# First round of turned attention scores: where the mask, the keys' products and the maxima's products stand around the turn of the row maxima

## The chip, the cores and the metric

The kernel runs on one core of a Trainium2 chip. The metric is the device time of one execution in microseconds (us), median of three runs. The engines are named as in the profile: PE is TensorE's matmul stream, PEld its weight loads, DVE VectorE, ACT ScalarE, POOL GpSimd, SP SyncE with its DMA queue.

## The reference

The program is a decoder of four layers on x of 8 batches x 256 tokens x 256 features, with a context of 8 x 77 x 256. Each layer adds an attention, a cross attention and a feed-forward part to x. The parts that the change touches are four softmax attentions with 16 heads each:

```python
def _local_attn(q, k, v, window):          # L1_attn, causal, 256 tokens (two windows of 128)
    ...
    sim = jnp.einsum('bnwd,bnkd->bnwk', qw, bk)
    sim = jnp.where(mask[None], sim, -1000000000.0)
    attn = jax.nn.softmax(sim, axis=-1)
    out = jnp.einsum('bnwk,bnkd->bnwd', attn, bv)

def _mha(xq, xk, xv, Wq, bq, Wk, bk, Wv, bv, Wo, bo, causal):   # L1_xattn
    ...
    w = jax.nn.softmax(scores, axis=-1)
    out = jnp.einsum('bhqk,bhke->bhqe', w, v)
    ...
h = _mha(x, x, x, Wq1, bq1, Wk1, bk1, Wv1, bv1, Wo1, bo1, causal=True)
out = _mha(h, encoder_k, encoder_v, Wq2, bq2, Wk2, bk2, Wv2, bv2, Wo2, bo2, causal=False)
```

L2_xattn is a plain cross attention to the 77 context rows. L3_xattn is the same on features of 32 per head, exp(z) and exp(-z) side by side.

## The kernel before, in words

Each engine has one program written out by hand; what joins them are semaphores. The stages follow each other as L0_attn, L0_xattn with L0_ffn, L1_attn, L1_xattn with L1_ffn, L2_attn, L2_xattn, L2_ffn with L3_attn, L3_xattn, L3_ffn. An attention stage works in steps, one batch (256 tokens, two tiles of 128) each; L1_xattn has 16 steps, 8 causal ones (the self attention, called a) and 8 cross ones (b), in the order a0 a1 a2 b0 a3 b1 a4 b2 a5 b3 a6 b4 a7 b5 b6 b7. In a step p the engines work on `now` (scores and softmax), `last` (outputs of the step before), `soon` (projections of the next one).

What a step does for its softmax, in this order:

- Scores with the queries on the partitions, `pair_scores_tensor` (L515 for the mask, L531, L537, L545, L552 for the products), two rounds for a cross step and three for a causal one, in the four PSUM banks HI to HI+3. After each round DVE takes the row maxima, `pair_tops_vector` (L567), and raises `top`. These scores are then overwritten.
- DVE splits the maxima into three bf16 parts in four short operations, `split_tops_vector` (L576 to L582), each of which raises `part`.
- PE turns the parts with two transposes, `turn_tops_tensor` (L590), ACT copies the result from PSUM to SBUF as mT, `turn_tops_scalar` (L597).
- PE computes the scores again, now with the keys on the partitions, in the same four banks, `turned_scores_tensor`, again two or three rounds. A round consists of the mask (causal only, four matmuls of 128x512 in bf16, L515 through `hide_later`), and for each `place` (one of the four heads of a group, with its columns) four small matmuls on four row groups that subtract the maxima (`k.pick` x mT in bf16, L606, "the maxima's products") and four that multiply keys and queries in f32 (L613, "the keys' products"). Round 0 of a causal step has four places of 128 columns, a round of a cross step two places of 256 columns. After the round `t_ps` is raised and ACT takes the exponential of all four banks at once, `turned_probs_scalar` (L648), which raises `prob`. The next round waits for it, as its banks are the same.
- PE multiplies with the values, `pair_outputs_tensor` (L660, L665), ACT copies (L673), PE turns the outputs back (L682), DVE divides (L692, L694, raises `o`), PE turns them again (L701) and projects them (L414, the shared projection helper).

Around the place of the change, PE's order in the four stages is this. L1_attn: own_k for `soon`, then the turn and round 0, then the second half of the feed-forward's first product, round 1, own_v for `soon` (DVE's L761 waits for it, and behind it DVE has the two layernorms of `last`, L1954 to L1967). L1_xattn: pair_back (L682), the turn and round 0, then, if `soon` is causal, own_v (which waits for DVE's L724, the keys of `soon`) and the query, else L701 and the query; then round 1. L2_xattn: L682, turn, round 0, L701 (waits for `o` of L694), query, round 1. L3_xattn: L4132, turn, round 0, L4206 (waits for `o` of L4198), a value projection, round 1; later L4147 waits for ACT's L4179.

Signals: `after(pe, s, u, name, i)` waits for the i-th raising of `name` of step u. PE executes in order, so that everything behind a wait stands still.

Of the kernel before, what the change touches and what calls it, by code (L numbers as in the profile page):

```python
# [22 lines left out]
P = 128  # L23
B, SEQ, D = 8, 256, 256
TILES = B * SEQ // P
SPARE = 4
KC = D // P
CTX = 77
# [151 lines left out]
def cut(ap, **sizes):  # L180
    (name, n), = sizes.items()
    return ap.rearrange(f"p ({name} f) -> p {name} f", **{name: n})
# [313 lines left out]
def keys_of(s, u):  # L496
    return s.kT[u.at][:, :, 0:2 * (SEQ if u.a.causal else CTX)]


def after(eng, s, u, name, i=1):  # L500

    if u is not None:
        eng.wait_ge(*s.sig.at(u.a.p + name, 0, u.n, i))


def group(i):
    return slice(PAD * i, PAD * (i + 1))
# [89 lines left out]
    k.nc.scalar.activation(s.mT, k.ps[:, b, at:at + P].bitcast(BF16), ACT.Copy).then_inc(*s.sig.up(u.a.p + "mT"))  # L597


def turned_pair(k, s, u, c, q, keys, at, fresh):  # L600

    n = q.stop - q.start
    for ab in (0, 1):
        j, out = 2 * c + ab, slice(at + ab * n, at + (ab + 1) * n)
        for i in range(4):
            k.nc.tensor.matmul(k.ps[0:u.a.nk, HI + i, out], k.pick[group(i), j * P:j * P + u.a.nk], s.mT[group(i), q],  # L606
                               start=fresh, stop=False, skip_group_check=True)
        if u.a.wide:
            kT, qT = s.kT[u.at][:, j, keys], s.qT[u.at][:, j, q]
        else:  # L610
            kT, qT = cut(keys_of(s, u)[:, c, :], half=2)[:, ab, keys], s.qT[u.at][:, c, q]
        for i in range(4):
            ins = k.nc.tensor.matmul(k.ps[0:u.a.nk, HI + i, out], kT[group(i)], qT[group(i)], start=False, stop=True,  # L613
                                     skip_group_check=True)
    return ins


def turned_scores_tensor(k, pe, s, u, r):

    if r == 0:  # L620
        after(pe, s, u, "mT")
    else:
        after(pe, s, u, "prob", r)
    every, later, first, second = slice(0, SEQ), slice(P, SEQ), slice(0, P), slice(P, SEQ)
    if not u.a.causal:
        ins = turned_pair(k, s, u, r, every, slice(0, CTX), 0, True)
    elif r == 0:
        for i in range(4):
            hide_later(k, k.ps[:, HI + i, :], mask_of(k, "keyC"))
        for c in range(KC):  # L630
            ins = turned_pair(k, s, u, c, later, second, c * SEQ, False)
    else:
        for i in range(4):
            hide_later(k, cut(k.ps[:, HI + i, :], slot=4)[:, 0::2, :], mask_of(k, "keyC")[:, 0:2 * P])
        ins = turned_pair(k, s, u, r - 1, every, first, 0, False)
    ins.then_inc(*s.sig.up(u.a.p + "t_ps"))


# [218 lines left out]
def L2_xattn_tensor(k, pe, s):  # L857
    for p in range(B + 1):
# [19 lines left out]
            logits_tensor(k, pe, s.ahead, 0, 0, 4)  # L878
        if now:
            after(pe, s, soon, "zT")  # L880
            turn_tops_tensor(k, pe, s, now, 3)
            turned_scores_tensor(k, pe, s, now, 0)
        if last:
            after(pe, s, last, "o")
            after(pe, s, soon, "kv")
# [230 lines left out]
def L1_xattn_tensor(k, pe, s):  # L1116
    quant, _, _ = fp8_times(s)
    ends, one = len(s.steps) - 1, s.ahead
    for p in range(ends + 1):
# [29 lines left out]
        if now:  # L1149
            if soon and soon.a.causal:  # L1150
                after(pe, s, soon, "zT")
            if p in quant:
                experts(pe, s, quant[p], "zT")
            turn_tops_tensor(k, pe, s, now, 3)
            turned_scores_tensor(k, pe, s, now, 0)
        if p == ends:
            step_z_tensor(k, pe, one, 1, 3)
        if soon and soon.a.causal:
# [878 lines left out]
def L1_attn_tensor(k, pe, s):  # L2037
# [3 lines left out]
    for p in range(B + 2):  # L2041
# [26 lines left out]
        if now:  # L2068
            if older:
                after(pe, s, older, "f", 1)  # L2070
            turn_tops_tensor(k, pe, s, now, 2)
            turned_scores_tensor(k, pe, s, now, 0)
        if p == B:
            pe.wait_ge(*k.loaded["L1_xattn"])
            own_k_tensor(k, pe, one, own, HI + 1)
# [2135 lines left out]
def L3_xattn_tensor(k, pe, s):  # L4211
# [4 lines left out]
    for p in range(B + 1):  # L4216
# [26 lines left out]
        if p == 0:  # L4243
            scan_z_tensor(k, pe, scan, B - 1)
        if now:
            turn_tops_tensor(k, pe, s, now, 3, 384)
            turned_scores_tensor(k, pe, s, now, 0)
        if p == 0:
            scan_ab_tensor(k, pe, scan, B - 1)
        if last:  # L4250
# [775 lines left out]
```

## Time and profile before

| | before |
|---|---|
| median of 3 runs (lowest, highest) | 3287.49 us (3282.52, 3294.82) |
| span of the profiled execution | 3285.4 us |
| mean granted TensorE clock | 0.950 |
| PE busy | 2996.5 us (91%), 20671 instructions |
| DVE busy | 1884.9 us (57%) |
| ACT busy | 1236.1 us (38%) |
| POOL busy | 453.8 us (14%) |

The profiled execution is one run; of its time only the span from the first to the last instruction is given, so the span stands for both. A busy share is an average over all stages. The turns of the row maxima that the change touches stand between 1156 and 3153 us: 8 in L1_attn, 16 in L1_xattn, 8 in L2_xattn, 8 in L3_xattn.

### The profile page before, as it was taken

The numbers are of one execution on the slowest core, as the hardware profiler recorded it, in microseconds if no ns is written. First come the engines' busy times: TensorE is split into PE (matmuls) and PEld (weight loads), VectorE is DVE, ScalarE is ACT, GpSimd is POOL, SyncE is SP. The second block draws the span as 40 slices with busy tenths as digits, with TensorE's granted clock in tenths as the row PEclk, the third lists the DMA queues.
The fourth block names the chain that finished last, engine by engine and source line by source line (L and its number), as shares of the span: only waits on it lengthen the run. The fifth ranks groups of instructions, "written<-read, shape, count | busy, mean of one in ns | idle before, by whom it ended". The sixth has DMA issues, their size and how long they took to land.

```text
span 3285.4 us, 52265 instructions
## 1 busy us (share of the span) xinstructions
PE 2996.5 (91%) x20671; PEld 1989.7 (61%) x20671; DVE 1884.9 (57%) x6444; ACT 1236.1 (38%) x1935; POOL 453.8 (14%) x470
## 2 busy tenths in 40 slices
PE   7999999988998888888888799997999999998988
PEld 4766657855554555555555456565666677765653
DVE  5444343799989256665676867674244444334455
ACT  2212222345555432223333458643333333223443
POOL 0010101123433300000010236510000000000000
PEclk9999999989998999989999769998999999998999
DMA  3000000010000100000000011000000000000000
GB/s 124 1 1 1 1 1 1 1 51 1 1 1 1 56 8 1 1 5 1 1 1 1 18 34 27 19 31 26 0 1 0 1 1 1 1 1 1 9 1 26
DMA packets 22029, 37.76 MB, mean 11 GB/s; under 512 B 2132, under 2 KB 19733, under 8 KB 20760
## 3 DMA queue, kind: packets, MB, share of 16 engines
q1 hardware_dynamic: 20968, 34.02, 3.0%
q8 instruction: 163, 2.67, 0.3%
q14 instruction: 82, 0.67, 0.1%
q10 hardware_dynamic: 816, 0.39, 0.0%
HBM read 26.81 MB, written 2.10 MB: 9 GB/s over the span
## 4 chain that ended last, share of the span: by engine, by line
PE 74%; DVE 18%; ACT 5%; issue 2%; DMA 0%; DVEq 0%; SPq 0%; POOL 0%; ACTq 0%; POOLq 0%
PE ps L414 43%; DVE arena L567 4%; PE ps L613 3%; ACT arena L648 2%; PE ps L2996 2%; PE ps L515 2%; PE ps L2304 2%; PE ps L3015 2%; PE ps L2258 2%; PE ps L1534 2%; PE ps L701 2%; PE ps L660 2%; DVE arena L1872 1%; PE ps L552 1%; PE ps L2869 1%
## 5 line engine op out<-in xcount | busy, mean ns | idle before, releaser
L414 PE MATMUL ps<-weights,arena 128*128 128x256 f32 (+4 forms) x2480 | 701.1, 432 | 21.0 <-ACT arena L1681 5.6
L414 PEld LDWEIGHTS ps<-weights,arena 128*128 128x128 f32 (+1 forms) x2480 | 466.7, 199 | 188.1 <-issue 92.9
L414 PE MATMUL ps<-arena,weights 128*128 128x256 f32 (+4 forms) x1726 | 563.4, 475 | 14.7 <-DMA weights<-in_w_L_attn 6.0
L414 PEld LDWEIGHTS ps<-arena,weights 128*128 128x128 f32 (+1 forms) x1726 | 319.8, 193 | 220.5 <-issue 155.3
L414 PE MATMUL ps<-arena 128*128 128x256 f32 (+4 forms) x1618 | 428.1, 418 | 6.0 <-ACT arena L4531 1.5
L414 PEld LDWEIGHTS ps<-arena 128*128 128x128 f32 (+2 forms) x1618 | 298.8, 188 | 116.6 <-issue 76.0
L648 ACT ACTIVATE arena<-ps 77x2048 f32<-77x2048 f32 (+1 forms) x112 | 209.9, 1875 | 171.7 <-PE ps L613 156.9
L567 DVE TENSOR_REDUCE arena<-ps 128x16 f32<-128x1232 f32 (+2 forms) x96 | 179.0, 1865 | 153.7 <-PE ps L552 50.4
L829 POOL TENSOR_TENSOR x<-x,weights 128x512 f32<-128x512 f32 x32 | 43.8, 1369 | 1244.0 <-DVE arena L795 1196.4
L1872 DVE MATCH_REPLACE8 arena<-arena 128x77 f32<-128x77 f32 x1024 | 214.5, 226 | 0.0
L2271 ACT ACTIVATE arena<-ps 128x1536 f32<-128x1536 f32 x128 | 185.7, 1452 | 73.3 <-PE ps L2260 66.9
L2289 POOL TENSOR_SCALAR_AFFINE_SELECT arena<-arena 128x512 f32<-128x512 f32 x128 | 144.1, 1126 | 138.8 <-ACT arena L2271 138.3
L1865 DVE MAX8 arena<-arena 128x8 f32<-128x77 f32 x1024 | 154.0, 227 | 0.2 <-DVE rstd L280 0.2
L701 PE MATMUL ps<-ident,arena 128*128 128x128 f32 x544 | 95.7, 303 | 49.2 <-POOL arena L1908 14.9
L3963 DVE COPY arena<-ps 128x1024 f32<-128x1024 f32 x16 | 19.6, 1224 | 203.4 <-PE ps L414 203.4
L613 PE MATMUL ps<-arena 32*77 32x256 f32 (+2 forms) x1792 | 132.4, 396 | 0.0
L2280 DVE TENSOR_TENSOR arena<-arena 128x512 f32<-128x512 f32 x128 | 90.0, 703 | 72.4 <-ACT arena L2271 71.6
L701 PEld LDWEIGHTS ps<-ident,arena 128*128 128x128 f32 x544 | 64.9, 151 | 95.5 <-issue 46.2
L3874 ACT ACTIVATE arena<-ps 128x512 f32<-128x512 f32 x128 | 76.5, 597 | 119.6 <-PE ps L414 119.5
L515 PE MATMUL ps<-masks,identb 128*128 128x256 bf16 (+1 forms) x384 | 79.5, 333 | 45.5 <-DVE arena L567 24.6
L660 PE MATMUL ps<-arena 77*17 77x256 f32 (+2 forms) x1536 | 108.1, 385 | 8.0 <-ACT arena L648 8.0
L2258 PE MATMUL ps<-arena 32*128 32x256 bf16 x512 | 111.3, 293 | 2.6 <-DMA arena<-arena 2.6
(410 smaller groups left out, 4517.5 us busy)
## 6 DMA issues: line engine op xcount, KB each, us to landing
arena<-arena SPq DMA_DIRECT2D x156, 32.0 KB
weights<-in_w_L_ffn SPq DMA_DIRECT2D x1, 3848.0 KB, 11.5
weights<-in_w_L_attn SPq DMA_DIRECT2D x1, 3840.0 KB, 15.3
weights<-in_w_L_xattn SPq DMA_DIRECT2D x3, 1024.0 KB, 6.4
weights<-in_w_L_ffn SPq DMA_DIRECT2D x1, 3072.0 KB, 9.9
x<-in_x SPq DMA_DIRECT2D x2, 1024.0 KB
weights<-in_w_L_xattn SPq DMA_DIRECT2D x1, 2048.0 KB, 7.4
out<-x SPq DMA_DIRECT2D x8, 256.0 KB, 2.2
```

The lines of the kernel that those rows point to most:

```text
L414: ins = k.nc.tensor.matmul(out, lhsT, rhs, start=start and i == 0, stop=i == n - 1)
L515: k.nc.tensor.matmul(out, k.identb[:, :], mask, start=True, stop=False, skip_group_check=True)
L567: k.nc.vector.tensor_reduce(out, src, AX, ALU.max).then_inc(*s.sig.up(u.a.p + "top"))
L613: ins = k.nc.tensor.matmul(k.ps[0:u.a.nk, HI + i, out], kT[group(i)], qT[group(i)], start=False, stop=True, skip_group_check=True)
L648: k.nc.scalar.activation(out, k.ps[0:u.a.nk, HI:HI + 4, :], ACT.Exp, scale=u.a.scale)\
L660: ins = k.nc.tensor.matmul(k.ps[PAD * i:PAD * i + u.a.vw, LO + c, at:at + SEQ], v[0:nk, 0, 4 * j + i, :], s.prob[0:nk, i, j * SEQ:(j + 1) ...
L701: ins = k.nc.tensor.transpose(out[:, (2 * c + t) * P:(2 * c + t + 1) * P], src[:, t, c * P:(c + 1) * P], k.ident[:, :])
L1865: ins = k.nc.vector.max(tops, left)
L1872: ins = k.nc.vector.match_replace(left, tops, left, -BIG)
L2258: mm(k.ps[:, base + u // 2, u % 2 * SEQ:(u % 2 + 1) * SEQ], kk[:, 0:P], q, start=True, stop=True, skip_group_check=True)
L2271: k.nc.scalar.activation(s.prob[at % PROBS], k.ps[:, base:base + 3, :].rearrange("p b f -> p (b f)"), ACT.Exp, scale=NH1 ** -0.5).then_inc ...
L2289: k.nc.gpsimd.affine_select(diag, diag, [[0, 4], [1, P]], ALU.is_ge, 0.0, base=0, channel_multiplier=-1)\
```

## The change

`turned_pair` is taken apart into `turned_products` (keys' products) and `turned_maxima` (maxima's products); `turned_places` lists the places of a round. A new `turned_first_tensor` does the turn and round 0 together. Its order on PE is: wait for the last `top`; the four mask matmuls (causal) or the keys' products of the first place (cross); wait for the fourth `part` and the two transposes; the keys' products of the other places (all four in a causal step); wait for mT; the maxima's products of all places. In a cross step only the first place's keys' products start the accumulation. Rounds 1 and 2 keep their order. L1_attn, L1_xattn, L2_xattn and L3_xattn call it in the place of `turn_tops_tensor` and `turned_scores_tensor(..., 0)`; the L0 stages keep their own. ACT's, DVE's, POOL's and SP's programs are unchanged.

```diff
--- before.py
+++ after.py
@@ -597,42 +597,67 @@
     k.nc.scalar.activation(s.mT, k.ps[:, b, at:at + P].bitcast(BF16), ACT.Copy).then_inc(*s.sig.up(u.a.p + "mT"))
 
 
-def turned_pair(k, s, u, c, q, keys, at, fresh):
-
-    n = q.stop - q.start
-    for ab in (0, 1):
-        j, out = 2 * c + ab, slice(at + ab * n, at + (ab + 1) * n)
-        for i in range(4):
-            k.nc.tensor.matmul(k.ps[0:u.a.nk, HI + i, out], k.pick[group(i), j * P:j * P + u.a.nk], s.mT[group(i), q],
-                               start=fresh, stop=False, skip_group_check=True)
-        if u.a.wide:
-            kT, qT = s.kT[u.at][:, j, keys], s.qT[u.at][:, j, q]
-        else:
-            kT, qT = cut(keys_of(s, u)[:, c, :], half=2)[:, ab, keys], s.qT[u.at][:, c, q]
-        for i in range(4):
-            ins = k.nc.tensor.matmul(k.ps[0:u.a.nk, HI + i, out], kT[group(i)], qT[group(i)], start=False, stop=True,
-                                     skip_group_check=True)
+def turned_places(u, r):
+
+    every, later, first, second, own = slice(0, SEQ), slice(P, SEQ), slice(0, P), slice(P, SEQ), slice(0, CTX)
+    if not u.a.causal:
+        return [(2 * r + ab, every, own, ab * SEQ) for ab in (0, 1)]
+    if r == 0:
+        return [(j, later, second, j * P) for j in range(4)]
+    return [(2 * r - 2 + ab, every, first, ab * SEQ) for ab in (0, 1)]
+
+
+def turned_products(k, s, u, place, fresh, stop):
+
+    j, q, keys, at = place
+    c, ab, out = j // 2, j % 2, slice(at, at + q.stop - q.start)
+    if u.a.wide:
+        kT, qT = s.kT[u.at][:, j, keys], s.qT[u.at][:, j, q]
+    else:
+        kT, qT = cut(keys_of(s, u)[:, c, :], half=2)[:, ab, keys], s.qT[u.at][:, c, q]
+    for i in range(4):
+        ins = k.nc.tensor.matmul(k.ps[0:u.a.nk, HI + i, out], kT[group(i)], qT[group(i)], start=fresh, stop=stop,
+                                 skip_group_check=True)
     return ins
 
 
-def turned_scores_tensor(k, pe, s, u, r):
-
-    if r == 0:
-        after(pe, s, u, "mT")
-    else:
-        after(pe, s, u, "prob", r)
-    every, later, first, second = slice(0, SEQ), slice(P, SEQ), slice(0, P), slice(P, SEQ)
-    if not u.a.causal:
-        ins = turned_pair(k, s, u, r, every, slice(0, CTX), 0, True)
-    elif r == 0:
+def turned_maxima(k, s, u, place, fresh, stop):
+
+    j, q, _, at = place
+    for i in range(4):
+        ins = k.nc.tensor.matmul(k.ps[0:u.a.nk, HI + i, at:at + q.stop - q.start],
+                                 k.pick[group(i), j * P:j * P + u.a.nk], s.mT[group(i), q], start=fresh, stop=stop,
+                                 skip_group_check=True)
+    return ins
+
+
+def turned_first_tensor(k, pe, s, u, b, at=0):
+
+    after(pe, s, u, "top", u.a.rounds)
+    causal, places = u.a.causal, turned_places(u, 0)
+    if causal:
         for i in range(4):
             hide_later(k, k.ps[:, HI + i, :], mask_of(k, "keyC"))
-        for c in range(KC):
-            ins = turned_pair(k, s, u, c, later, second, c * SEQ, False)
     else:
+        turned_products(k, s, u, places[0], True, False)
+    turn_tops_tensor(k, pe, s, u, b, at)
+    for place in places if causal else places[1:]:
+        turned_products(k, s, u, place, False, False)
+    after(pe, s, u, "mT")
+    for place in places:
+        ins = turned_maxima(k, s, u, place, False, True)
+    ins.then_inc(*s.sig.up(u.a.p + "t_ps"))
+
+
+def turned_scores_tensor(k, pe, s, u, r):
+
+    after(pe, s, u, "prob", r)
+    if u.a.causal:
         for i in range(4):
             hide_later(k, cut(k.ps[:, HI + i, :], slot=4)[:, 0::2, :], mask_of(k, "keyC")[:, 0:2 * P])
-        ins = turned_pair(k, s, u, r - 1, every, first, 0, False)
+    for place in turned_places(u, r):
+        turned_maxima(k, s, u, place, not u.a.causal, False)
+        ins = turned_products(k, s, u, place, False, True)
     ins.then_inc(*s.sig.up(u.a.p + "t_ps"))
 
 
@@ -878,8 +903,7 @@
             logits_tensor(k, pe, s.ahead, 0, 0, 4)
         if now:
             after(pe, s, soon, "zT")
-            turn_tops_tensor(k, pe, s, now, 3)
-            turned_scores_tensor(k, pe, s, now, 0)
+            turned_first_tensor(k, pe, s, now, 3)
         if last:
             after(pe, s, last, "o")
             after(pe, s, soon, "kv")
@@ -1151,8 +1175,7 @@
                 after(pe, s, soon, "zT")
             if p in quant:
                 experts(pe, s, quant[p], "zT")
-            turn_tops_tensor(k, pe, s, now, 3)
-            turned_scores_tensor(k, pe, s, now, 0)
+            turned_first_tensor(k, pe, s, now, 3)
         if p == ends:
             step_z_tensor(k, pe, one, 1, 3)
         if soon and soon.a.causal:
@@ -2068,8 +2091,7 @@
         if now:
             if older:
                 after(pe, s, older, "f", 1)
-            turn_tops_tensor(k, pe, s, now, 2)
-            turned_scores_tensor(k, pe, s, now, 0)
+            turned_first_tensor(k, pe, s, now, 2)
         if p == B:
             pe.wait_ge(*k.loaded["L1_xattn"])
             own_k_tensor(k, pe, one, own, HI + 1)
@@ -4243,8 +4265,7 @@
         if p == 0:
             scan_z_tensor(k, pe, scan, B - 1)
         if now:
-            turn_tops_tensor(k, pe, s, now, 3, 384)
-            turned_scores_tensor(k, pe, s, now, 0)
+            turned_first_tensor(k, pe, s, now, 3, 384)
         if p == 0:
             scan_ab_tensor(k, pe, scan, B - 1)
         if last:
```

## Rows read from the trace of the kernel before

**Rows 1.** The page, part 4: the chain that ended last.
```profile
PE 74%; DVE 18%; ACT 5%; issue 2%; DMA 0%; DVEq 0%; SPq 0%; POOL 0%; ACTq 0%; POOLq 0%
```

**Rows 2.** PE's waits by line: us in total, times, longest us.
```profile
PE ps L590 <- DVE arena L582: 42.0, 27, 4.6
...
PE ps L606 <- ACT arena L597: 11.4, 24, 0.5
...
PE ps L515 <- ACT arena L597: 7.6, 16, 0.5
```

**Rows 3.** Timeline, one L1_attn turn: start us, us, engine, line [idle before <-releaser].
```profile
1282.54 2.29 DVE L567 TENSOR_REDUCE arena<-ps 128x8 f32<-128x2048 f32 x1 [1.80 <-PE ps L552]
...
1283.33 1.89 PE L414 MATMUL ps<-arena,weights 128*128 128x256 f32 x8
...
1285.57 0.23 DVE L582 TENSOR_TENSOR arena<-arena 128x32 bf16<-128x32 f32 x1
...
1285.94 0.27 PE L590 MATMUL ps<-identb,arena 128*128 128x128 bf16 x2 [0.72 <-DVE arena L582]
...
1286.69 1.04 PE L515 MATMUL ps<-masks,identb 128*128 128x512 bf16 x4 [0.48 <-ACT arena L597]
...
1287.66 0.10 PEld L606 LDWEIGHTS ps<-arena,pick 32*128 32x128 bf16 x4 [0.42 <-issue]
...
1289.10 1.99 PE L414 MATMUL ps<-arena,weights 128*128 128x256 f32 x8
...
1294.95 0.69 DVE L761 TENSOR_TENSOR arena<-ps,weights 128x512 f32<-128x512 f32 x1 [6.37 <-PE ps L414]
```

**Rows 4.** Timeline, one causal step of L1_xattn (a1).
```profile
1488.35 1.09 PE L682 MATMUL ps<-ident,arena 128*128 128x128 f32 x8
1488.49 2.29 DVE L567 TENSOR_REDUCE arena<-ps 128x8 f32<-128x2048 f32 x1
...
1491.89 0.27 PE L590 MATMUL ps<-identb,arena 128*128 128x128 bf16 x2 [2.44 <-DVE arena L582]
...
1496.28 2.34 PE L414 MATMUL ps<-weights,arena 128*128 128x256 f32 x8
```

**Rows 5.** The same turn by windows: us, busy by engine, granted clock, DMA.
```profile
1491.00:1492.00 1.00, 0.11 (x2) 0.13 (x2) 0.90 (x10) 0.00 (x0) 0.00 (x0) 1.00 0.00 0
...
1495.00:1496.00 1.00, 1.00 (x28) 0.94 (x20) 0.61 (x1) 0.00 (x0) 0.00 (x0) 0.50 0.00 0
```

**Rows 6.** Timeline, causal step a6 of L1_xattn behind its round 0.
```profile
1705.65 6.56 DVE L966 TENSOR_SCALAR arena<-arena 128x512 f32<-128x512 f32 x1
...
1714.44 2.81 PE L414 MATMUL ps<-weights,arena 128*128 128x256 f32 x8 [1.89 <-DVE arena L1302]
```

**Rows 7.** Timeline, cross step b1 of L1_xattn, followed by a causal one.
```profile
1588.30 1.90 DVE L724 TENSOR_SCALAR arena<-ps,cols 128x256 f32<-128x256 f32 x4
1588.64 0.28 PE L590 MATMUL ps<-identb,arena 128*128 128x128 bf16 x2
...
1590.60 1.99 PE L414 MATMUL ps<-weights,arena 128*128 128x256 f32 x8
```

**Rows 8.** Timeline, one step of L2_xattn.
```profile
2155.71 0.69 DVE L694 TENSOR_TENSOR arena<-ps,arena 128x512 f32<-128x512 f32 x1
...
2156.46 0.66 PE L701 MATMUL ps<-ident,arena 128*128 128x128 f32 x4 [0.25 <-DVE arena L694]
```

**Rows 9.** Timeline, one step of L3_xattn.
```profile
3054.29 0.29 PE L590 MATMUL ps<-identb,arena 128*128 128x128 bf16 x2 [0.44 <-DVE arena L582]
...
3056.41 1.87 ACT L648 ACTIVATE arena<-ps 77x2048 f32<-77x2048 f32 x1 [1.41 <-PE ps L613]
...
3060.35 1.13 PE L4147 MATMUL ps<-arena,weights 64*128 64x256 f32 x8 [0.74 <-ACT arena L4179]
```

**Rows 10.** Timeline, the last step of L2_xattn: the turn and the exponential.
```profile
2243.47 0.29 PE L590 MATMUL ps<-identb,arena 128*128 128x128 bf16 x2 [1.50 <-DVE arena L582]
...
2246.41 1.87 ACT L648 ACTIVATE arena<-ps 77x2048 f32<-77x2048 f32 x1 [2.23 <-PE ps L613]
```

## The prediction

> **What bounds the kernel now.** First the page's chain that ended last: three quarters of it is PE, a fifth DVE [rows 1]. PE is the bound on average, but not where this change acts, so the next view is PE's list of waits by line. The longest entry of all is the transposes L590 that wait for the last split of the maxima (L582), and close behind L590 stand the waits of L515 and L606 for mT [rows 2]. These three hold 42.0 + 11.4 + 7.6 = 61.0 us of PE's idle time, a small part of it (8 of 48 turns) in L0 stages that stay as they are. The waits alone don't say whether the time is lost for good, so I read the timeline around the turns: what PE does before the turn, what stands ready, and who waits for round 0. There are 40 turns, in five patterns.
>
> **L1_attn (8 turns).** own_k ends on PE at 1285.22; the last maxima are ready at 1284.83, the split at 1285.80. PE idles 0.72, turns, idles 0.48 until mT is back (0.75 from the start of the turn to the start of the masks), does the masks (0.97 to the next weight load) and round 0's products (1.44), and is free at 1289.10 [rows 3]. All of the masks and the keys' products need only `top`. After the change: masks from 1285.22 or a hair later, 0.97; transposes 0.10; keys' products, which I take as two thirds of the 1.44 (four f32 passes against one bf16, but short groups), about 0.95, longer than the 0.75 of mT's way; the maxima's products 0.5. Sum 2.5 to 2.6, so PE is free at 1287.8, 1.3 earlier. The turn itself starts later than before (about 1286.3 against 1285.94); that is covered, because mT's way is now hidden by the keys' products. Who waits: the exponential, round 1 behind it, own_v, and DVE's L761, which has stood idle for 6.37 us and has the whole chain of layernorms and the next step's first maxima queued behind it [rows 3]. So the 1.3 goes through, step after step. In the first two turns PE comes to the turn later than the split and less is won (0.6 to 0.8), the last has the pattern of the next paragraph but partly runs into DVE. I take 9.8 for the stage; the bounds are 5 (if DVE's chain keeps half) and 12.
>
> **L1_xattn, causal (8 turns).** Here PE is done with L682 at 1489.44 while DVE takes the third maxima until 1490.78, and PE stands still for 2.44 us, then for mT [rows 4]. After that the granted clock falls from 1.00 to 0.50, the lower of its two levels [rows 5]. From the turn's start to the next stage's work it takes 4.39 (1491.89 to 1496.28) [rows 4], where the same work at the full clock took 3.16 (1285.94 to 1289.10) [rows 3]; 1.23 us are the clock's. After the change the masks fill 1490.85 to 1491.8, so that the turn starts where it did (the split ends at 1491.75), and behind it come 0.10 + 0.95 + 0.5 = 1.55: PE is free at 1493.45 instead of 1496.28, 2.8 us earlier, 1.6 of them by order alone and 1.2 by the clock. The idle stretch shrinks from 2.44 + 0.48 to about 1.4, and I count on the clock staying up. Behind the turn everything is serial: exponential, round 1, exponential, round 2, exponential, next step's scores. What PE does beside the first exponential also ran partly at the low clock, so that some turns give more than 2.8; I take 3.2 for six of them, 2.3 for a0 (a longer stand before the maxima, so the clock falls anyway), and 0 for a6: there DVE's L966 took 6.56 us and PE's L414 stood for the copy behind it (L1302) [rows 6], a chain that begins at the split and not at round 0. Sum 21.5. Bounds: 1.6 each if the clock falls anyway (6 x 1.6 + 1 = 10.6), and 27 with a6 freed.
>
> The Trainium skill (TensorE: Matmul & The Clock Gate, part 1) says that the monitor behind the gate runs freely, so that the same kernel finds its cold matmuls at other places from run to run. This trace shows one run only and neither bears it out nor not; by that rule a turn may stay at the low clock although its idle time is shorter, and it is the first rival below that prices this from rows.
>
> **L1_xattn, cross (8 turns).** PE comes later than the split, so only mT's way can be filled. In the new order one place's keys' products stand ahead of the transposes: the turn is 0.4 later, the second place's products cover part of mT's 0.75, and round 0 ends about 0.5 earlier. But what follows is own_v, which waits for DVE's L724, done at 1590.20; L414 started at 1590.60 [rows 7]. So 0.33 for five turns, 1.6 together. b5 and b6 have the split late as in L3_xattn below (0.9, and some clock): 2.8. b7 gives nothing, DVE's chain is what ends last there. Sum 4.4, bounds 2 and 6.
>
> **L2_xattn (8 turns).** Six turns gain nothing: L701 behind round 0 starts at 2156.46, when L694 has just ended (2156.40) [rows 8], and L694 hangs on DVE's own order behind the split. The exponential would be half a us earlier, but round 1 stands behind L701 and the query on PE. The first turn has no `last` and gives 0.6; the last had 1.50 us idle, then the low clock, and 2.94 from the turn to the exponential, which is on the path [rows 10], against 2.12 in L3_xattn's like turn at the full clock [rows 9]: 1.6. Sum 2.2, bounds 0.5 and 5.
>
> **L3_xattn (8 turns).** PE waits 0.44 for the split and the turn starts at 3054.29; the exponential starts 2.12 later [rows 9]. Both places' keys' products (twice the columns of a causal place, so about 0.45 each) now lie in the two waits: the turn stays where it was, the exponential comes 0.86 earlier. Behind it ACT is nearly without a gap until L4179, for which PE's L4147 has waited 0.74 [rows 9], so that the 0.86 goes through. Six times 0.86, 0.9 in the last and 1.6 in the first (low clock, products at double length in the waits): 7.7, bounds 4 and 9.
>
> **Costs of the edit.** No instruction is added but one wait on `top` per turn, for which PE otherwise waited through `part`: nothing, or at most the 0.05 or so per turn that separates a release from its waiter (2 us in all). Nothing moves on the DMA queues. The f32 products of several places now follow each other without a bf16 group between; the trace has no round 0 of this form, and between no change and one more weight load of 0.10 per place [rows 3] (40 turns, 112 places at most: 5 us if nothing hid it, and in half the turns the wait for mT hides it) I take no change, as loads run beside products throughout.
>
> **The sum.** 9.8 + 21.5 + 4.4 + 2.2 + 7.7 = 45.6 us. Not every turn's successors were followed to the end of the stage; DVE holds a fifth of the chain [rows 1], and I take off a tenth: 41 us. The profiled execution (3285.4) stands 2.1 under the median of the runs shown (3287.49), so the forecast is 3287.5 - 41 = 3246.
>
> **The rivals.**
>
> *The clock is not given back.* The low stretches stay behind the causal turns, merely later. For it: about 1.4 us of idle time remain. Against it: L3_xattn and L1_attn have waits of 0.44 to 0.72 and mT's beside each other at the full clock [rows 3, 9]. Price: 1.2 to 1.6 in each of six turns, and about 2 in the others with a low clock: the gain is 31, the time 3256.
>
> *The gain is swallowed by DVE.* In L1_attn or L1_xattn DVE has less slack than its idle time before L761 suggests, or the layernorm and fp8 chains become the wait of most steps as L1302 is in a6. Price: half of the sum, 20 us, time 3267.
>
> *No change to tell.* All that is left is L3_xattn's and a few turns: under 16 us, time about 3277.
>
> *Slower.* The one mechanism that could do it is the clock: with round 0 done earlier, PE stands longer for the exponentials and for `o`, and falls to the low clock in turns where it did not. One such fall costs about 1.2 us as in a1 [rows 3, 4]; against 41 us of gain it decides from about 34 new falls in 40 turns. Time then 3305 at worst. Little speaks for it: PE's total idle time shrinks.
>
> **How the numbers follow.** Forecast 0.60, clock not given back 0.17, swallowed 0.15, no change 0.05, slower 0.03. The likeliest case's own range is 3238 to 3254; upward the range takes in the next two rivals, downward the upper bounds of the terms (12 + 27 + 6 + 5 + 9 = 59): 3230 to 3268. Half a per cent, 16 us, is about what a measurement of this kernel can tell from no change. Faster by more than that: 0.60 + 0.17 + 0.15 and nothing of the rest, 0.92; within: 0.05; slower: 0.03.
>
> **What the profile after would show.** Step by step: L590's wait for L582 falls from 42 to under 20 us, and the waits for mT all but vanish in causal steps and stay at 0.2 in cross steps that come late; L515 stands ahead of L590, L613 on both sides of it in cross steps; from the turn to the next L414 1.6 in L1_attn instead of 3.16; windows behind the turns of a1 to a7 read 1.00. The distance between turns shrinks by 1.3 in L1_attn, by 3 over a causal step of L1_xattn, by 0.9 in L3_xattn, and stays in L2_xattn. Wrong would make it: a clock of 0.50 still behind the turns (first rival), DVE's L761, or in L1_xattn the residual sum behind round 2, without idle time before it (second), or f32 products that take more than 0.25 per place of 128 columns when they follow each other.

## The result, and the profile after

| | before | after |
|---|---|---|
| median (lowest, highest) | 3288.16 us (3282.52, 3294.82), 4 runs | 3242.14 us (3240.72, 3246.36), 4 runs |
| ratio, 95% interval | | 0.9852 (0.9839 to 0.9866) |
| span of the profiled execution | 3285.4 us | 3239.2 us |
| mean granted TensorE clock | 0.950 | 0.956 |
| PE, DVE busy | 2996.5, 1884.9 us | 2979.7, 1885.2 us |

46.0 us faster between the medians, 46.2 between the spans; forecast 41, from a sum of 45.6. The lines have moved: keys' products L613 are now L619, maxima's products L606 are L628, the exponential L648 is L673, L724 is L749, L966 is L990, L1302 is L1325; L590, L597, L567, L582 and L515 are where they were.

PE's waits, by line (total, times, longest), beside [rows 2]: first one more line of before, then the lines of after.

```profile
PE ps L515 <- DVE arena L567: 24.6, 25, 2.4
```

```profile
PE ps L515 <- DVE arena L567: 39.8, 35, 2.9
...
PE ps L414 <- DVE arena L1325: 5.9, 2, 5.2
...
PE ps L619 <- DVE arena L567: 5.4, 4, 4.3
...
PE ps L590 <- DVE arena L582: 2.7, 4, 1.1
```

The wait of 42.0 us for the split has fallen to 2.7, and the waits for mT are gone from the list, but 39.8 us now stand in front of the masks L515, for the maxima themselves. Line L515 also makes the masks of the first scores, where the same wait was 24.6 us before and is 25.2 now. At the turns 14.6 us stand in front of the masks (nine turns), 5.4 in front of the first place's products (four) and 2.7 in front of the transposes: 22.7 us in all, for the 61.0 of before. So the list shows 38 us gone and some 20 under another name, and a wait named anew is not time won. (All 61.0 us of before stood at these 40 turns, none of them in an L0 stage.) What was won is seen behind the wait, as the timeline of the L1_attn turn of [rows 3] shows:

```profile
1278.25 2.29 DVE L567 TENSOR_REDUCE arena<-ps 128x8 f32<-128x2048 f32 x1 [1.80 <-PE ps L552]
...
1280.78 1.03 PE L515 MATMUL ps<-masks,identb 128*128 128x512 bf16 x4
...
1281.64 0.28 PE L590 MATMUL ps<-identb,arena 128*128 128x128 bf16 x2
...
1281.84 1.17 PE L619 MATMUL ps<-arena 32*128 32x128 f32 x32
1281.95 0.38 ACT L597 ACTIVATE arena<-ps 128x256 bf16<-128x256 bf16 x1 [4.54 <-PE ps L590]
...
1282.84 0.40 PE L628 MATMUL ps<-arena,pick 32*128 32x128 bf16 x16
...
1283.17 1.99 PE L414 MATMUL ps<-arena,weights 128*128 128x256 f32 x8
```

From the turn to the next L414 it is 1.53 us, where [rows 3] had 3.16. The keys' products cover all of mT's way (ACT's L597 and the time around it). And the turn stands 1.10 behind the end of the maxima (1280.54), as before (1.11): the masks fitted into the time for which PE had waited for the split anyway.

The causal turn a1, beside [rows 4], and its windows (length, busy share of PE, PEld, DVE, ACT and POOL, granted clock, DMA), beside [rows 5]:

```profile
1473.82 2.29 DVE L567 TENSOR_REDUCE arena<-ps 128x8 f32<-128x2048 f32 x1
...
1476.25 1.02 PE L515 MATMUL ps<-masks,identb 128*128 128x512 bf16 x4 [1.48 <-DVE arena L567]
...
1477.12 0.28 PE L590 MATMUL ps<-identb,arena 128*128 128x128 bf16 x2
...
1478.33 0.40 PE L628 MATMUL ps<-arena,pick 32*128 32x128 bf16 x16
1478.67 1.99 PE L414 MATMUL ps<-weights,arena 128*128 128x256 f32 x8
```

```profile
1477.00:1478.00 1.00, 1.00 (x25) 0.78 (x26) 0.93 (x11) 0.38 (x1) 0.00 (x0) 1.00 0.00 0
1478.00:1479.00 1.00, 1.00 (x38) 0.87 (x31) 0.83 (x6) 0.22 (x1) 0.00 (x0) 1.00 0.07 16
```

From the turn to the next L414 it is 1.55, where it was 4.39. The clock stays at 1.00. From the turn to the exponential it is 1.66 in all eight causal turns; before it was 4.54 to 5.49.

The cross turn b1, beside [rows 7]:

```profile
1563.78 1.90 DVE L749 TENSOR_SCALAR arena<-ps,cols 128x256 f32<-128x256 f32 x4
...
1564.21 0.67 PE L619 MATMUL ps<-arena 32*77 32x256 f32 x8
...
1564.82 0.28 PE L590 MATMUL ps<-identb,arena 128*128 128x128 bf16 x2
...
1565.57 0.42 PE L628 MATMUL ps<-arena,pick 32*77 32x256 bf16 x8
...
1565.92 1.35 PE L414 MATMUL ps<-weights,arena 128*128 128x256 f32 x5
```

Here the turn comes 0.70 later behind the end of the maxima (1.91 for 1.21), and from the turn to the exponential it is 0.88 shorter, so that the exponential comes 0.18 earlier.

Following all 40 turns through both traces gives where the time went (the time from one turn's start to another's, before less after):

| stretch | gained | forecast |
|---|---|---|
| start of the program to the first turn (nothing changed but that turn itself) | -2.9 | 0 |
| L1_attn, first turn to L1_xattn's first | 11.8 | 9.8 |
| L1_xattn, first turn to last | 30.9 | 25.9 |
| L2_attn, up to L2_xattn's first turn | -2.6 | 0 |
| L2_xattn, first turn to last | 1.3 | 2.2 |
| last turn of L2_xattn to first of L3_xattn | 3.4 | 0 |
| L3_xattn, first turn to the end | 4.4 | 7.7 |

Their sum is 46.2. In the second trace of the changed kernel (below) the first line is +0.5 instead of -2.9, and L1_xattn 27.5 instead of 30.9. These two lines are the uncertain ones. The first turn of the 13 traces of this study starts at 1156.3 to 1165.4, although the work ahead of it is the same in all of them. And the stretch of L1_xattn takes 351.5 to 361.3 us in four traces that have the old order and the clears as before (357.6 in the trace of before), and 326.7 to 332.8 in three with the new order. The means differ by 26.2 us. In L1_attn and L3_xattn the traces with the same order agree within 0.4 us, but for one that is 2.1 shorter in L1_attn. One step stands out. Between a6's turn and b4's the changed kernel takes 26.08 us, where the four like steps take 18.45 each, and the kernel before took 24.24: the only step that got longer. In the timeline behind a6's turn, beside [rows 6]:

```profile
1672.72 1.39 POOL L854 TENSOR_TENSOR x<-x,weights 128x512 f32<-128x512 f32 x1 [40.20 <-DVE arena L820]
1673.01 6.57 DVE L990 TENSOR_SCALAR arena<-arena 128x512 f32<-128x512 f32 x1
...
1674.04 1.81 POOL L2707 MEMSET arena<- 128x2048 f32 x1
...
1675.78 3.51 POOL L2708 MEMSET arena<- 128x4096 bf16 x1
...
1679.24 3.79 POOL L2709 MEMSET arena<- 128x4096 bf16 x1
...
1679.61 0.69 DVE L991 TENSOR_TENSOR arena<-arena 128x512 f32<-128x512 f32 x1
```

L990 takes 6.57 us, while L1000 of the same shape takes 0.43, and it ends 0.29 after one of GpSimd's clears (memsets) does. Those clears belong to L2_attn and start as soon as GpSimd is free. PE waits 5.15 us at the end of this chain, and then works for five to six us at the low clock:

```profile
1681.81 2.50 PE L414 MATMUL ps<-weights,arena 128*128 128x256 f32 x5 [5.15 <-DVE arena L1325]
```

```profile
1683.00:1684.00 1.00, 1.00 (x4) 0.82 (x3) 0.93 (x3) 0.00 (x0) 0.03 (x1) 0.50 0.00 0
```

### The profile page after: what moved, and what is told of

Read it like the earlier page. It is cut to its first block, busy times and chain, and to the rows that moved or that the text cites. A ratio compares the mean times of both kernels' runs of the same rounds, so it can differ in the third digit from the quotient of the medians.

```text
span 3239.2 us, 52265 instructions
## 1 busy us (share of the span) xinstructions
PE 2979.7 (92%) x20671; PEld 1975.9 (61%) x20671; DVE 1885.2 (58%) x6444; ACT 1236.1 (38%) x1935; POOL 453.1 (14%) x470
## 4 chain that ended last, share of the span: by engine, by line
PE 75%; DVE 18%; ACT 4%; issue 2%; DMA 0%; DVEq 0%; SPq 0%; POOL 0%; ACTq 0%; POOLq 0%
PE ps L414 43%; DVE arena L567 3%; PE ps L619 2%; ACT arena L673 2%; PE ps L3018 2%; PE ps L2326 2%; PE ps L3037 2%; PE ps L2280 2%; PE ps L1557 2%; PE ps L515 2%; PE ps L726 2%; PE ps L685 2%; DVE arena L1895 1%; PE ps L552 1%; PE ps L2891 1%
## 5 line engine op out<-in xcount | busy, mean ns | idle before, releaser
L414 PE MATMUL ps<-weights,arena 128*128 128x256 f32 (+4 forms) x2480 | 703.7, 433 | 25.0 <-ACT arena L1704 5.6
L414 PEld LDWEIGHTS ps<-weights,arena 128*128 128x128 f32 (+1 forms) x2480 | 467.4, 199 | 192.0 <-issue 92.5
L414 PE MATMUL ps<-arena,weights 128*128 128x256 f32 (+4 forms) x1726 | 565.5, 476 | 14.8 <-DMA weights<-in_w_L_attn 6.1
L414 PEld LDWEIGHTS ps<-arena,weights 128*128 128x128 f32 (+1 forms) x1726 | 320.3, 193 | 220.9 <-issue 156.3
L414 PE MATMUL ps<-arena 128*128 128x256 f32 (+4 forms) x1618 | 426.6, 417 | 6.0 <-ACT arena L4552 1.5
L414 PEld LDWEIGHTS ps<-arena 128*128 128x128 f32 (+2 forms) x1618 | 298.1, 188 | 115.6 <-issue 75.1
L567 DVE TENSOR_REDUCE arena<-ps 128x16 f32<-128x1232 f32 (+2 forms) x96 | 179.0, 1865 | 149.7 <-PE ps L552 52.3
L673 ACT ACTIVATE arena<-ps 77x2048 f32<-77x2048 f32 (+1 forms) x112 | 210.0, 1875 | 107.8 <-PE ps L619 64.2
L854 POOL TENSOR_TENSOR x<-x,weights 128x512 f32<-128x512 f32 x32 | 43.8, 1371 | 1214.1 <-DVE arena L820 1165.1
L619 PE MATMUL ps<-arena 32*77 32x256 f32 (+2 forms) x1792 | 119.9, 366 | 5.4 <-DVE arena L567 5.4
L515 PE MATMUL ps<-masks,identb 128*128 128x256 bf16 (+1 forms) x384 | 75.0, 320 | 53.0 <-DVE arena L567 39.8
L726 PEld LDWEIGHTS ps<-ident,arena 128*128 128x128 f32 x544 | 63.1, 148 | 98.3 <-issue 45.6
```

Source lines behind the costliest of these rows:

```text
L414: ins = k.nc.tensor.matmul(out, lhsT, rhs, start=start and i == 0, stop=i == n - 1)
L515: k.nc.tensor.matmul(out, k.identb[:, :], mask, start=True, stop=False, skip_group_check=True)
L567: k.nc.vector.tensor_reduce(out, src, AX, ALU.max).then_inc(*s.sig.up(u.a.p + "top"))
L673: k.nc.scalar.activation(out, k.ps[0:u.a.nk, HI:HI + 4, :], ACT.Exp, scale=u.a.scale)\
L726: ins = k.nc.tensor.transpose(out[:, (2 * c + t) * P:(2 * c + t + 1) * P], src[:, t, c * P:(c + 1) * P], k.ident[:, :])
```

## The experiments

My theory: the gain is order (work moved into waits, on the path) plus a clock that no longer falls, stage by stage additive. Rivals: the clock falls anyway or explains most; one stage's gain is swallowed. For the experiments the new function takes an order for each stage, and parts of its code are left out below at each `...`.

**One stage at a time.** Four kernels in which only one stage has the new order and the others have the old. For L1_attn alone:

```diff
+ORDER = {'L1_attn': 'new', 'L1_xattn': 'old', 'L1_xattn_c': 'old', 'L2_xattn': 'old', 'L3_xattn': 'old'}
```

> The new order in L1_attn alone, the order of before in the other stages. My theory (each stage keeps what its turns give, and the parts add): the turns of L1_attn come 1.7 us closer per step as in the changed kernel, 10 to 12 us less than before, about 3277 us. The rival (a stage's gain is lost at the next stage's first waits unless that stage is shortened too): less than 6 us.

> The new order in L1_xattn alone. My theory: 26 to 31 us less than before, about 3259 us, of which 2 to 3 are given back in L2_attn as in the changed kernel. The rival (parts don't add): under 20 us.

> The new order in L2_xattn alone. My theory: the six middle turns give nothing because the transposes L701 wait for DVE's o, the first and the last give 2 us together: 3286 us, not to be told from before by the times; the distances between the middle turns stay at 14.5 us. The rival (round 0 sets the step): 0.9 us in each of 8 turns, 7 us less.

> The new order in L3_xattn alone. My theory: 0.8 us per step as ACT's chain behind the exponential sets the step, 6 to 8 us less, about 3281 us. The rival (the gain of 5 us between the first and the last turn is all, the ends give it back): 4 us or less.

| only in | median | before beside it | ratio, 95% interval | gained between the turns of the stage, profiled execution |
|---|---|---|---|---|
| L1_attn | 3275.25 | 3290.34 | 0.9947 (0.9934 to 0.9961) | 11.7 |
| L1_xattn | 3264.90 | 3290.34 | 0.9926 (0.9913 to 0.9938) | 24.8 |
| L2_xattn | 3287.21 | 3290.34 | 0.9990 (0.9980 to 0.9999) | 1.3 |
| L3_xattn | 3286.48 | 3290.34 | 0.9990 (0.9980 to 0.9999) | 4.4 |

The four ratios multiply to 0.9854, the whole change has 0.9852: within their intervals the parts add, and no stage swallows another's gain. Three of the four missed what was expected. L1_attn alone gave 15.1 us by the medians for 10 to 12, L1_xattn alone 25.4, just under the 26 to 31. L3_xattn alone gave 3.9 by the medians and 4.4 behind its first turn, where 6 to 8 had been expected: there the rival came true, that the ends give a part back. In L3_xattn each distance between middle turns is 19.02 for 19.81, exactly the 0.79 by which the exponential comes earlier, counted from the end of the maxima. In L2_xattn the middle ones stay at 14.53 to within 0.01. L1_xattn alone moves its turns by 24.8, 6.1 less than in the whole change (30.9): 3.1 of that is again the step behind a6, which takes 29.18 there, and 3.0 the step from a0 to a1, where a low stretch is left.

**Three other orders in all four stages**, to part order and clock. The first, "ahead", has the head (masks or the first place's keys' products) ahead of the turn and all else behind mT; the second, "behind", has nothing ahead of the turn, and behind it the head and the keys' products, then, after mT, the maxima's; the third, "filled", only lets PE work on the masks in the long wait, and then does them once more where they stood, so that a causal round 0 is as long as before and only the idle time is broken:

```python
    if mode in ("new", "ahead", "filled"):
        after(pe, s, u, "top", u.a.rounds)
        head()              # masks (causal) or the first place's keys' products (cross)
    turn_tops_tensor(k, pe, s, u, b, at)
    if mode == "behind":
        head()
    if mode in ("new", "behind"):
        ...                 # the other keys' products, wait for mT, maxima's products
    else:
        after(pe, s, u, "mT")
        if mode in ("old", "filled") and causal:
            head()
        ...                 # place by place: maxima's products, then keys' products
```

> Half of the change: the masks (causal) or the first place's keys' products (cross) stand ahead of the turn, but behind the turn PE waits for mT before it does anything else, then all other products. Order theory: a causal turn wins the masks' 0.97 less the later turn (0.6 in L1_attn, 1.0 in L1_xattn), a turn of L3_xattn 0.45, in all 16 us. With the clock given back behind a1 to a7 by the shorter idle stretch (1.4 before the masks, 0.5 behind the turn) 8 to 10 us more: about 3264 us. If the clock stays low there: about 3272 us.

> The other half: the turn comes first, as soon as the split is done, and masks and all keys' products stand between the turn and mT, the maxima's products last. Order theory: every turn wins about 0.65 to 0.8 where it is on the path (mT's way is covered), 16 to 20 us in all: about 3270 us. The idle stretch of 2.44 us ahead of the turn stays in L1_xattn; the clock theory says the clock still falls to its lower level behind a1 to a7, so that no more than that is won. If the clock did not come from that stretch, it stays up and the time is 3260 us or less.

> The order of before, with idle time filled by work done twice: the masks (causal) or the first place's keys' products (cross) are issued ahead of the turn and then once more at their old place, so that nothing useful is moved. Clock theory: the low stretch behind a1 to a7, u7 and the last turns of L2_xattn goes away and gives 1.2 to 1.6 us each, 10 to 14 us, less 3 to 5 us for turns that now come later (L1_attn 0.35 each, the cross steps where PE is late 0.45 each): 6 to 10 us less than before, about 3280 us. The rival (order alone, the clock gives nothing): 3 to 5 us more than before, about 3292 us.

| order | median | before | ratio, 95% interval | causal turns of L1_xattn, turn to exponential |
|---|---|---|---|---|
| ahead | 3271.05 | 3290.33 | 0.9940 (0.9925 to 0.9956) | 2.34 in two, 3.2 to 3.6 in six |
| behind | 3267.68 | 3290.33 | 0.9927 (0.9913 to 0.9941) | 2.50 in two, 3.3 to 4.1 in six |
| filled | 3283.21 | 3290.33 | 0.9982 (0.9973 to 0.9991) | 3.32 in six, 4.9 in two |

"Ahead" and "filled" came out a few us above what the clock given back would have made of them (3264 and 3280 expected), "ahead" at the time expected for a clock that stays low (3272). In each order the shortest value is that of turns at the full clock; the longer ones ran in part at the low clock. A low one in "ahead", the turn a2 (1513.6), by windows:

```profile
1515.00:1516.00 1.00, 1.00 (x28) 0.93 (x20) 0.18 (x1) 0.00 (x0) 0.74 (x1) 0.50 0.06 16
1516.00:1517.00 1.00, 1.00 (x20) 0.79 (x16) 0.00 (x0) 0.00 (x0) 0.52 (x1) 0.50 0.00 0
```

and a1 in "filled" (turn at 1487.97):

```profile
1489.00:1490.00 1.00, 1.00 (x16) 0.46 (x18) 0.83 (x6) 0.00 (x0) 0.00 (x0) 1.00 0.00 0
1490.00:1491.00 1.00, 1.00 (x44) 0.99 (x40) 0.86 (x5) 0.00 (x0) 0.00 (x0) 1.00 0.00 0
```

"Filled" has the old round 0 behind mT, and a1 took 3.32 from turn to exponential instead of 4.54: the difference of 1.22 is the clock alone, the size that the prediction had read from [rows 3, 4]. It lasted in six of eight turns. Between the turns of a0 and b3 "filled" gained 7.4 us, the changed kernel 22.9. So about a third of the gain there can be had from the clock alone. As an estimate of the clock's share this is rough: "filled" let the clock fall in two of these six causal turns and also delays the cross turns, and the same unchanged stretch was 1.1 us shorter than before with only L1_attn changed and 1.4 longer with only L2_xattn changed. The whole kernel gained 7.1 by the medians; in its cross turns the exponential came 0.7 later, since there nothing was saved for the product put ahead of the turn. With either half of the new order alone the clock still fell in six of eight causal turns, and with both halves in none of the changed kernel (in the kernel with L1_xattn alone, in a0: 2.81). So neither half alone keeps the clock up in most turns.

**GpSimd's clears.** The step behind a6 needs a cause. The edit holds the three clears until a6's fp8 step is through, in the changed kernel and in the kernel before; a third kernel adds the order "behind" for the cross turns that PE reaches late; the fourth is the changed kernel once more:

```diff
 def L2_attn_gpsimd(k, pool, s):
     p, x = k.nc.gpsimd, s.behind
+    experts(pool, x, fp8_times(x)[0][10], "q")
     p.memset(s.blank[0], 0.0)
```

> The changed kernel, with one wait more: GpSimd's three clears for L2_attn start behind the fp8 step of a6 (its q), not as soon as GpSimd is free. Theory (the clears hold up DVE's tensor_scalar L990, 6.57 us in the profile after against 0.43 for a like one, L1000): L990 takes 0.43, the step from a6's turn to b4's takes 18.5 as the four like steps of this stage do (18.45) and not 26.08, and the kernel gains up to 7.6 us over the changed one: 3234.5. Rival (the step is long because of what is special in a6, DVE's fp8 chain ahead of L1325): the step stays near 26 and the time near 3242. Another: the clears, now at most 9 us behind the fp8 step, hold up the next tensor_scalars (L1104) instead, and half is lost.

> The kernel before with the same wait alone. If the clears held up L966 (6.56 us) there too, the step from a6's turn to b4's falls from 24.24 to the 21.0 of the like steps: 3.2 us, time 3285. With 7.6 in the changed kernel and 3.2 here, the clears took 4.4 us of the change's gain. Rival: no change.

> The changed kernel with the wait for the clears, and with the turn first, then both places' keys' products, then the maxima's, in the cross turns to which PE comes later than the split (b0 to b4, c0 to c6); all others as in the changed kernel. From the runs of the one order and of the other: about 0.1 us over each of five steps of L1_xattn, about 1 in c0, nothing in c1 to c6: 1.5 us under the kernel with the wait alone, 3233; hardly to be told from it by the time, by the distance between turns it is.

> The changed kernel once more, beside the three others on the same chip: 3242, for their comparison; a second trace of the same program, in which the distances between turns agree with the first, and the stretches of low clock, if they come from the program alone, lie at the same places.

| kernel | median | ratio to before (3290.91), 95% interval | a6's turn to b4's | fp8 tensor_scalar in a6 |
|---|---|---|---|---|
| changed, clears later | 3231.80 | 0.9827 (0.9809 to 0.9844) | 18.45 | 1.38 |
| before, clears later | 3287.73 | 0.9987 (0.9978 to 0.9996) | 20.91 | 1.37 |
| mixed orders, clears later | 3232.89 | 0.9826 (0.9810 to 0.9842) | 17.75 | 1.38 |
| changed, again | 3241.92 | 0.9855 (0.9837 to 0.9874) | 29.48 | 10.02 |

The changed kernel with the clears later, behind a6's turn:

```profile
1670.69 1.38 POOL L854 TENSOR_TENSOR x<-x,weights 128x512 f32<-128x512 f32 x1 [40.19 <-DVE arena L820]
1670.98 1.38 DVE L990 TENSOR_SCALAR arena<-arena 128x512 f32<-128x512 f32 x1
...
1676.85 1.81 POOL L2708 MEMSET arena<- 128x2048 f32 x1 [4.78 <-DVE arena L1001]
...
1679.03 0.75 DVE L1104 TENSOR_SCALAR arena<-ps,arena 128x512 bf16<-128x512 f32 x1 [1.65 <-PE ps L414]
```

The changed kernel once more, with the clears where they were (its lines stand 27 further down):

```profile
1669.26 1.38 POOL L881 TENSOR_TENSOR x<-x,weights 128x512 f32<-128x512 f32 x1 [40.20 <-DVE arena L847]
1669.55 10.02 DVE L1017 TENSOR_SCALAR arena<-arena 128x512 f32<-128x512 f32 x1
1670.59 1.80 POOL L2734 MEMSET arena<- 128x2048 f32 x1
1672.33 3.51 POOL L2735 MEMSET arena<- 128x4096 bf16 x1
1675.79 3.51 POOL L2736 MEMSET arena<- 128x4096 bf16 x1
```

In the first trace of this program the tensor_scalar came through after the second clear (6.57 us), here after the third (10.02). In the ten traces with the clears where they were it is 6.56 or 6.57 in four, the kernel before among them, and 10.01 to 10.03 in six. With the clears held back it still takes 1.38 and not the 0.43 that was expected, for it then waits for GpSimd's own L854; the median of its nine executions is 0.43. Each time it ended 0.27 to 0.29 after a GpSimd operation. The theory holds, the rival (something special in a6's fp8 chain) falls: the step is as short as its four likes. The step lost more than the tensor_scalar did (7.6 us for 5.2 in the first trace, 11.0 for 8.6 in the second). The other 2.4 us fit the low clock behind PE's wait of 5.15 or 8.60 us: with the clears held back PE stands for 0.36 there and the windows read 1.00. L1104, which runs beside the clears now, reads PSUM and takes the same 0.75 as before. The medians of the first and fourth kernel differ by 10.1 us; their intervals overlap a little, but the 11.0 us of the step in their traces account for it. (One of the five runs of the first kernel took 3240.1, the other four 3231.0 to 3232.0.) In the kernel before the same edit gives 3.3 us in the profiled execution (24.24 to 20.91) and 3.2 by the medians.

The mixed kernel: c0 comes 1.06 us earlier than in the first one, and where the steps from a4 on have 41.39 us for a pair instead of 41.57, the step before a3 has 1.3 more for a reason that I did not look for. Over all it can't be told apart. The best kernel of this study is the changed one with the clears later, 3231.8 us.

## Why the prediction was right

**Total.** Sum 45.6, measured 46.0 by the medians. Taking off a tenth for chains not followed was not needed. But that 45.6 met 46.0 is partly luck. Against their terms L1_attn gave 2.0 more, L1_xattn 5.0 more (in one trace; 0.3 more by the means above), L2_xattn 0.9 less and L3_xattn 3.3 less, and the three stretches put at nothing came to -2.9, -2.6 and 3.4.

**L1_attn, 9.8 forecast, 11.8 measured.** Mechanism right, size off: the term "1.3 earlier" per turn measured 1.67, counted here and below from the end of the maxima to the exponential. The step that failed is "the turn itself starts later than before (about 1286.3 against 1285.94)": it starts no later, because the masks behind own_k took 0.7 from its end to the transposes, not 0.97. Keys' products took 1.17 where I had taken 0.95, but their end overlaps the maxima's (0.40 for 0.5), so that from turn to next stage it is 1.53, forecast 1.6. The first two turns, forecast at 0.6 to 0.8 each, gave 1.2 to 1.5. In the last, u7, the exponential came 3.3 earlier, but a0's turn followed 0.75 later than before (63.4 for 62.7 from turn to turn): there the chain that ended last runs over DVE's layernorms, as the prediction had feared for this turn, and behind them PE ran at 0.50 from 1439 to 1445, where the low stretch before was 1449 to 1453.

**L1_xattn, causal.** "2.8 per turn, 1.6 by order and 1.2 by the clock": the exponential came 3.0 to 3.9 earlier. The order's 1.6 and the clock's 1.2 are both confirmed for a1 (2.98 in all, 1.22 of it clock by the order "filled"); a0 and a5 had had longer low stretches, and gave 3.9. For a0 I had expected a fall of the clock anyway and took 2.3; it stayed up. The rival "the clock is not given back" did not happen here, but the orders "ahead" and "behind", in which it happened in six of eight turns, show that it was near.

**a6, 0 forecast.** The step was 1.8 longer in one trace of the changed kernel and 5.2 in the other, and 5.8 shorter with the clears held back. The prediction had the row [rows 6] with 6.56 us for L966 and reasoned correctly that the wait hangs on this chain. But a term of nothing had no room for the step to grow, by the clears and by the low clock behind the longer wait. What it didn't ask is why one tensor_scalar takes fifteen times what L976 of the same shape takes. The Trainium skill (SBUF — State Buffer, section "SBUF: two separate sides") says that DVE in some of its modes and GpSimd share one pair of ports, and that whoever has it keeps it for a whole instruction; the traces agree with it, in that the instruction took 1.38, 6.57 or 10.02 us and each time ended right behind a GpSimd operation. The ports themselves no trace shows: shown is that the clears cost the time, argued is by what.

**Cross turns.** "The turn is 0.4 later ... round 0 ends about 0.5 earlier" was 0.70 and 0.18: the first place's keys' products take 0.61 to the transposes, not 0.4. Since own_v hangs on DVE, what is left is less still: L749 ends at 1565.68 and the next L414 starts 0.24 later, where before it started 0.40 later (1590.60 behind 1590.20). So 0.16 per step was won, forecast 0.33. The steps behind b5 and b6 became 2.3 us shorter each, 4.7 together in place of 2.8, part of it clock.

**L2_xattn, 2.2 forecast, 1.3 inside the stage.** "Six turns gain nothing" holds to 0.02 us. The first turn, forecast +0.6, cost: the place ahead of the transposes delays it by 1.2, which is half of the 2.6 given back ahead of it. With the turn first (the mixed kernel) c0 comes 1.06 earlier. Of the rest, and of the 3.4 gained between L2_xattn and L3_xattn, where no code was changed, 1.7 fit c7's exponential, which came that much earlier, but the size is not settled: the same stretch gained 3.5 with only L2_xattn changed and 1.2 with the clears later.

**L3_xattn, 7.7 forecast, 4.4 measured.** The 0.86 per step measured 0.79, and went through, as forecast, from d2 on. The terms that failed are the ends. "1.6 in the first" gave 0.6, although its exponential came 1.24 earlier; why is open. Of the last turn's 0.9 nothing reached the end, and 0.8 more was lost behind it. That was the clock: up to the 16 matmuls L414 of the chain that ended last the 0.9 was still won (18.26 us behind the turn for 19.14), but they took 5.42 us in place of 3.73, first the piece before, then the piece after with one of its windows:

```profile
3171.89 3.73 PE ps L414 x16
...
3123.98 5.42 PE ps L414 x16
```

```profile
3125.00:3126.00 1.00, 1.00 (x4) 0.74 (x3) 0.14 (x1) 0.00 (x0) 0.00 (x0) 0.50 0.00 0
```

Before, the windows there read 1.00. All three other traces with the new order in L3_xattn that were compared (L3_xattn alone, clears later, the changed kernel again) have the same 5.42 at the same place, so it belongs to the order. This is the mechanism that the prediction named under "slower", a new fall of the clock where there was none: it came once here, at 1.7 us, and once behind a6.

**What the profile after was to show.** L590's wait for the split was to be under 20 us and is 2.7. From the turn to L414 in L1_attn it was to be 1.6 and is 1.53. The clock is 1.00 behind the turns of a1 to a7, as forecast. The distance between turns shrank by 1.7 in the middle of L1_attn instead of 1.3, by 2.5 from most causal turns to the next cross turn, which itself comes 0.7 later (forecast 3), by 0.8 in L3_xattn, and not at all in the middle of L2_xattn.

## What to carry to other kernels

Split a fused group by what each part waits for, and put the part whose inputs are early into the wait of the other; what counts is not the wait that disappears from the list (here 20 of 61 us stood under another name afterwards) but the time from the release to the consumer's start. Where an engine reaches such a place late, anything put ahead of the released work delays it, so the order is chosen by who arrives last. And when one instruction takes many times what its like takes, look at what every other engine does in that time before costing the step at nothing: here that row was worth 10 us in the changed kernel, a fifth as much as the whole change. A shorter wait can also cost: look for stretches of low clock that are new, not only for those that have gone.

## What the runs showed of the hardware

- A DVE tensor_scalar on f32 in SBUF (0.43 us alone) stood behind 1, 3 or 4 GpSimd operations in a row, and took 1.38, 6.57 or 10.02 us. Tensor_tensors of f32 on DVE (0.69) beside the same clears were not slowed. Whether it gets in between two clears differs from execution to execution: the step took 26.08 and 29.48 in two traces of the changed kernel, and 22.62, 22.62, 24.24 and 28.23 in four of kernels with the old order there. That alone is 3 to 6 us of spread, as much as the smallest effects here.
- With idle times of 2.44 and 0.48 us on PE around the transposes (before), the granted clock fell behind seven of seven turns from a1 on; with 1.48 and 0.34, and no wait for mT, behind none. With 1.7 and 0.34 ahead and 0.48 behind the transposes it fell in two of eight ("filled", one of them a0, with 3.11 ahead), and in "ahead", with like waits and the same masks, in six: idle time around the turn alone doesn't tell the two apart, and what does stays open.
- Low-clock stretches also moved within unchanged code: with only L1_attn changed, the step to a3 took 1.2 us more than before, the one to b1 1.3 more and the one to b3 1.2 less. That L1_attn had become shorter is not the cause: with only L2_xattn changed, so that all code up to b7 is that of before, the same three steps took 1.3 more, 1.3 more and 1.2 less, while with only L3_xattn changed they took what they did before. The Trainium skill (TensorE: Matmul & The Clock Gate, part 1), whose rule of a freely running monitor the prediction weighed, agrees with that. It would also allow more than was seen in the new order, where two executions of the changed kernel agreed in the time from turn to exponential to 0.01 us in all 40 turns.
